# A Mamba and mixture-of-experts block on one core: who makes the products with C, and when ScalarE empties the banks of the last batch

## What is computed

```python
def _mamba_dir(xz, conv_w, conv_b, xproj_w, dtproj_w, dt_bias, A_log, Dp):
    ...
    dA = jnp.exp(jnp.einsum('bdl,dn->bdln', delta, A))
    dBx = jnp.einsum('bdl,bnl,bdl->bdln', delta, Bm, u)
    h = _ssm_scan(dA, dBx)
    y = jnp.einsum('bdln,bnl->bdl', h, Cm)
    y = y + Dp[None, :, None] * u
    return y * jax.nn.silu(z)
...
xz = jnp.einsum('ed,bld->bel', in_proj_w, hidden_states)
out_f = _mamba_dir(xz, ...)
out_b = _mamba_dir(xz[:, :, ::-1], ...)[:, :, ::-1]
attn = jnp.einsum('bdl,od->blo', out_f + out_b, out_proj_w)
...
w = jax.nn.softmax(topv, axis=-1)               # 4 of 16 experts for a token
hidden = jax.nn.gelu(jnp.einsum('bld,efd->blef', x, w1) + b1, approximate=False)
exp_out = jnp.einsum('blef,edf->bled', hidden, w2) + b2
fused = jnp.sum(w[..., None] * jnp.take_along_axis(exp_out, topi[..., None], axis=2), axis=2)
```

## Time and profile before

| | |
|---|---|
| median of 3 runs | 1203.09 us (1200.37 to 1204.73) |
| the profiled execution's own time | 1202.14 us |
| its span in the profile | 1200.2 us |
| mean granted TensorE clock | 0.925 |
| busy, share of the span | DVE 90%, PE 79%, ACT 76%, POOL 73% |
| DMA | 222.64 MB, 185 GB/s |

### The profile page before, as it was taken

The page is one execution under the profiler, slowest core; times in us unless marked ns, Lnnn a source line. Parts: engine busy times, 40 slices in busy tenths (PEclk is TensorE's granted clock), DMA queues, the critical chain, the costliest instruction groups (busy, mean ns, idle before and its releaser), DMA issues. The chain is left out here.

```text
span 1200.2 us, 21505 instructions
## 1 busy us (share of the span) xinstructions
PE 948.7 (79%) x5691; PEld 752.3 (63%) x5764; DVE 1083.1 (90%) x1402; ACT 910.8 (76%) x1647; POOL 874.9 (73%) x530
## 2 busy tenths in 40 slices
PE   5267788854789888988898888889888888897872
PEld 5133243323678767877777677777777767776762
DVE  7886788849999999999999989999999999698952
ACT  2037887777799987989898888889898987878720
POOL 1077868773579878987897788789878878785562
PEclk9987877776899999999999999999999998899985
DMA  9924445568556866776676668667766766554455
GB/s 314 325 82 156 176 154 218 186 250 294 178 168 170 228 184 168 199 198 178 162 218 185 190 151 228 166 170 201 203 171 165 230 177 170 141 146 144 118 108 152
DMA packets 151298, 222.64 MB, mean 185 GB/s; under 512 B 36028, under 2 KB 97756, under 8 KB 146276
## 3 DMA queue, kind: packets, MB, share of 16 engines
q1 hardware_dynamic: 124036, 202.16, 52.6%
q0 software_dynamic: 27136, 19.02, 11.1%
HBM read 159.74 MB, written 65.52 MB: 188 GB/s over the span
## 5 line engine op out<-in xcount | busy, mean ns | idle before, releaser
L748 POOL TENSOR_TENSOR arena<-arena 128x1024 f32<-128x1024 f32 x227 | 494.2, 2332 | 147.3 <-DVE arena L1390 131.7
L1390 DVE TENSOR_TENSOR_SCAN arena<-arena,ps 128x512 f32<-128x512 f32 x512 | 601.0, 1205 | 0.1
L934 ACT ACTIVATE arena<-delta,a_neg 128x511 f32<-128x511 f32 x512 | 338.2, 723 | 4.2 <-issue 2.2
L733 POOL DMA_INDIRECT acc_d<-yrows,tags x160 | 255.2, 1595 | 54.3 <-issue 36.1
L1083 PE MATMUL ps<-ident,arena 128*128 128x128 f32 x2048 | 275.8, 279 | 7.0 <-POOL arena L748 4.7
L1378 DVE TENSOR_TENSOR ps<-du,ps 128x512 f32<-128x512 f32 x384 | 253.8, 676 | 10.1 <-issue 5.8
L1083 PEld LDWEIGHTS ps<-ident,arena 128*128 128x128 f32 x2048 | 238.1, 144 | 17.6 <-POOL arena L748 4.7
L1112 PE MATMUL ps<-w,arena 128*128 128x128 f32 x1248 | 177.6, 286 | 10.5 <-DVE arena L1390 5.4
L715 POOL DMA_INDIRECT slots_d<-arena,pos x128 | 154.2, 1205 | 42.1 <-issue 40.6
L1104 PE MATMUL ps<-rowsT,w 128*128 128x256 f32 x640 | 159.1, 393 | 8.9 <-ACT arena L885 7.1
L1112 PEld LDWEIGHTS ps<-w,arena 128*128 128x128 f32 x1248 | 155.2, 194 | 15.1 <-ACT yrows L880 5.3
(11 more groups left out here) (141 smaller groups left out, 944.5 us busy)
## 6 DMA issues: line engine op xcount, KB each, us to landing
arena<-c_d SPq DMA_DIRECT2D x128, 512.0 KB
w<-w_dram SPq DMA_DIRECT2D x80, 258.0 KB
w<-w_dram SPq DMA_DIRECT2D x80, 256.0 KB
rows<-slots_d SPq DMA_DIRECT2D x80, 130.0 KB
slots_d<-delta SPq DMA_DIRECT2D x5, 2015.0 KB, 20.2
delta_d<-arena SPq DMA_DIRECT2D x8, 1024.0 KB
du_d<-delta SPq DMA_DIRECT2D x8, 1024.0 KB
delta<-delta_d SPq DMA_DIRECT2D x8, 1024.0 KB, 7.3
```

The source lines that it names most:

```text
L733: pool.indirect_dma_start(acc_d, bass.IndirectOffsetOnAxis(ap=tags[:, j, a, 0:1].bitcast(I32), axis=0), yrows[:, j % W_RING, a, :], None, ...
L748: nc.gpsimd.tensor_tensor(state[:, q % H_RING], state[:, q % H_RING], c_rows[:, r % C_RING], ALU.mult).then_inc(s["prod_done"], 1)
L934: nc.scalar.activation(decay[:, q % DA_RING, j, lo:lo + L - 1], delta[:, par, dh, lo:lo + L - 1], ACT.Exp, scale=a_neg[:, dh, 2 * g + j:2 ...
L1390: nc.vector.tensor_tensor_scan(state[:, q % H_RING, j, way], decay[:, q % DA_RING, j, way], b_ps[:, ROW[q, j], j, way], 0.0, ALU.mult, ALU ...
```

## The change

Three tables change, and one call is added.

- `VECTOR`: in a middle batch VectorE makes the product of pair 16 only, where it made those of pairs 8, 16 and 24.
- `LAST_VECTOR`: in the last batch VectorE makes the products of pairs 22 to 31, where it made those of 13, 16, 18, 20, 22, 24, 26 and 28. So that pair 31 can be among them, a call behind the loop over the pairs is added.
- `LAST_STEP`: in the last batch ScalarE empties the banks of TensorE's step p in step p+2, p+3 or p+4, where it was p+4 throughout (steps 12, 13, 24 and 25 are emptied within the GELU bursts, as before).

All other pairs' products are GpSimd's. The number of products, emptyings and sends stays what it was.

```diff
--- before.py
+++ after.py
@@ -58,8 +58,8 @@
 
 
 FIRST_VECTOR = (1, 4, 7)
-VECTOR = (8, 16, 24)
-LAST_VECTOR = (13, 16, 18, 20, 22, 24, 26, 28)
+VECTOR = (16,)
+LAST_VECTOR = tuple(range(22, 32))
 
 
 def vector_pairs(b):
@@ -158,7 +158,9 @@
 LAST_LAG = 4
 LAST_GELU = [16, 28]
 LAST_BURSTS = [[12, 13], [24, 25]]
-LAST_EMPTY = [[p for p in range(2, PAIRS) if p + LAST_LAG == q and p not in LAST_BURSTS[0] + LAST_BURSTS[1]]
+LAST_STEP = [p + (LAST_LAG - 2 if p < 6 or 15 < p < 19 else LAST_LAG - 1 if p < 9 or 13 < p < 22 or p == 26 else
+                  LAST_LAG - 2 if p > 26 else LAST_LAG) for p in range(PAIRS)]
+LAST_EMPTY = [[p for p in range(2, PAIRS) if LAST_STEP[p] == q and p not in LAST_BURSTS[0] + LAST_BURSTS[1]]
               for q in range(PAIRS + LAST_LAG)]
 
 
@@ -1419,6 +1421,8 @@
                     product(q + 2)
                     scan(q + 3, 0)
                     scan(q + 3, 1)
+                if isinstance(b, int) and b == BATCH - 1:
+                    product(PAIRS - 1)
 
             batch(0, 0, 0)
             batch(1, 1, 0)
```

## The result

The changed kernel takes 1166.84 us in the median of four runs (1161.03 to 1173.30); the kernel before took 1203.91 us beside it (1200.37 to 1205.13). The ratio is 0.972, with a 95% interval of 0.968 to 0.976: faster by 37 us. The forecast was 1164 us. The profiled execution of the changed kernel is the slowest of the four (1173.3 us, span 1170.8), so the two profiles differ by less than the medians: 1200.2 - 1170.8 = 29.4 us.

A forecast was written before the change was run, and what follows sets the result against it. VectorE was taken to bound the middle batches, chained scatters the end. 22.3 + 7.2 + 4.1 + 2.5 + 2.8 = 38.9 us off 1202.1 gives 1163.2, as median 1164; 8-in-10 range 1157 to 1181.

The forecast's parts named there:

- Removed products, 22.3 us: Six middle batches: VectorE loses the products of pairs 8 and 24, 1.14 + 2.58 us a batch, 22.3 us saved.
- The kept product, +7.2 us: Middle batches: pair 16's product on VectorE falls from 2.66 to 1.22 us in five batches, 7.2 us saved.
- VectorE comes first by 0.7 us, and the 1.44 us are not paid: Middle batches: VectorE starts pair 16's product at 6.2 us, before GpSimd is free for pair 15 at 6.9.
- an unfavourable phase: Last batch: a 4.33 us product showed that unfavourable phases could make the middle batches' kept product longer.
- Rival (a): Middle batches: the kept product goes on meeting GpSimd, 31.7 us gained in all, 1171 us; chance 0.28.
- TensorE and GpSimd follow at no cost: Middle batches: GpSimd's 98 us of work fits under VectorE's 103.6, TensorE's margin barely holds; the move costs nothing.
- Start of the last batch, 4.1 us: Before the last batch's gatings: earlier emptying gives 3.2 us, a kept clock up to 1.7 more; 4.1 taken.
- Middle of the last batch, 2.5 us: Last batch after the gatings: only TensorE's own gain counts, bounds 2.1 and 3.9 us, 2.5 taken.
- TensorE's wait under 3: Middle of the last batch: TensorE's wait of 4.69 us would fall to under 3 in the new profile.
- End of the last batch, 2.8 us: Last batch's sends: first 4.0 us later, third at 1127.7 instead of 1130.47, 2.8 us gained; bounds -1 and 6.
- every pair of sends 8 us apart: End of the last batch: each send waits for the one before to land, 8 us apart before and after.

The follow-up runs named there:

- the two halves' runs: mid_only and last_only, each one half of the change on the kernel before: 1183.63 us and 1187.40 us.
- again: The changed kernel run once more, unaltered: 1168.26 us, ratio 0.972 to the kernel before.
- kept_none: The changed kernel without any VectorE product in the middle batches, GpSimd makes all 32: 1148.40 us, ratio 0.953 to the kernel before.
- last_only: The changed kernel with the old VECTOR list (8, 16, 24), so only the last batch is changed: 1187.40 us, ratio 0.986 to the kernel before.
- mid_only: The kernel before with VECTOR = (16,), so only the middle batches are changed: 1183.63 us, ratio 0.983 to the kernel before.
- lv_only: The kernel before with only the new list of last-batch VectorE products (pairs 22 to 31): 1202.79 us, ratio 0.998 to the kernel before.
- ls_only: The kernel before with only the new LAST_STEP table (earlier evictions in the last batch): 1198.12 us, ratio 0.990 to the kernel before.
- kept_19: The changed kernel with the middle batches' remaining VectorE product moved from pair 16 to pair 19: 1157.35 us, ratio 0.965 to the kernel before.
- kept_8: The changed kernel with the middle batches' remaining VectorE product moved from pair 16 to pair 8: 1157.37 us, ratio 0.963 to the kernel before.
- no_reload: The changed kernel without SyncE's reload of the scans' sums beside the last sends: 1173.99 us, ratio 0.975 to the kernel before.

## Why the prediction was right, and where it was not

The direction, the bound (VectorE in the middle batches, the chain of sends at the end) and the total were right: 37 us measured, 38.9 forecast. Most of the terms were not.

**Removed products, 22.3 us: right.** Twelve products fewer; the two halves' runs and the group agree once the kept product is set apart.

**The kept product, +7.2 us: wrong, and this is the step that failed** ("VectorE comes first by 0.7 us, and the 1.44 us are not paid"). The arithmetic ahead of it came out in the fifth middle batch: VectorE issues the product 6.1 us behind the scans of pair 14 (854.86 to 861.00; forecast 6.2), GpSimd is free for pair 15 at 861.9, 7.0 behind (forecast 6.9). VectorE came first by 0.9 us there and by 0.7 at 645.99 (3.85 us long); in the other four batches it came 0.1 to 0.4 us after GpSimd had become free (2.67 to 2.97 us long), and in `again` it came first in all six, by 0.1 to 1.0. So the margin of 0.7 us was too thin to forecast the order by. Above all, coming first is not enough: the product behind GpSimd's scatter went ahead, and VectorE waited for the rest of the scatter and for all of it. The row that shows this, 4.33 us at 1086.10, was in the trace of before, and the prediction took it for an unfavourable phase. In place of a gain of 7.2 us the runs show a loss of 3.4 (19.4 instead of 16.0 us for six) to 6.0 (22.0). Rival (a), which had the product unchanged at 2.66, was nearer for this term and still too kind. The Trainium skill (SBUF — State Buffer, Who interferes with whom) says that two such instructions exclude each other for a whole instruction and that issue order decides. The exclusion agrees with every row here (1.1 us of VectorE's own work behind the end of GpSimd's product: 864.97 after 863.88); the order of issue that the rows list does not decide in the case at 861.00.

**TensorE and GpSimd follow at no cost: right.** Outside the loop's edge VectorE waits 1.1 us in six middle batches, and `kept_none` moves six more products to GpSimd without a wait of VectorE.

**Start of the last batch, 4.1 us (bounds 3.2 and 4.9): under-sized**, 6.6 in the profile. `last_only` has the same 2.5 us of idle time before the gatings, `mid_only` still 7.7, so it comes from the last batch's part of the change; of its two halves `lv_only`, which leaves the evictions as before, still has 8.3, and `ls_only` 5.0 in its one profile. TensorE's wait fell from 4.93 to 1.41 us, 3.5 (forecast 3.2). Most of the rest is the clock. TensorE's windows of the changed kernel there show the high level throughout, where before it was granted 0.50 for 3.4 us:

```profile
1022.00:1025.00 3.00, 1.59 (x15) 1.58 (x15) 3.00 (x5) 3.00 (x9) 3.00 (x2) 1.00 0.98 226
1025.00:1028.00 3.00, 3.00 (x26) 2.63 (x24) 0.62 (x2) 1.52 (x4) 2.86 (x2) 1.00 0.45 132
```

From the transpose to the second gating it takes 4.7 us instead of 7.0 (1023.42 to 1028.09, before 1042.69 to 1049.72), 2.4 us less. I had taken half of 1.7 us for the clock into the sum, and the 1.7 was itself too small. The last 0.7 us of the 6.6 I haven't traced.

**Middle of the last batch, 2.5 us (bounds 2.1 and 3.9): the clock decides.** The first profile gives 0.9, `again` 3.2 (second gating to the scans of pair 16, 51.8 us before, 50.9 and 48.6). Both have TensorE idle for 2.67 or 2.68 and then 0.68 us; in the first its clock then falls, in the second not. The same two gaps stand in four more profiles: the clock falls in `kept_19` and stays in `kept_8`, `kept_none` and `last_only`. The windows, first the changed kernel, then `again`:

```profile
1068.00:1072.00 4.00, 2.59 (x16) 2.33 (x16) 3.14 (x4) 3.26 (x7) 3.77 (x3) 0.79 0.49 150
1072.00:1076.00 4.00, 3.66 (x16) 3.51 (x17) 0.00 (x0) 0.66 (x2) 1.22 (x1) 0.50 0.59 185
```

```profile
1064.00:1068.00 4.00, 3.00 (x25) 2.84 (x26) 2.38 (x3) 3.17 (x7) 4.00 (x3) 1.00 0.41 140
1068.00:1072.00 4.00, 4.00 (x31) 3.71 (x29) 2.98 (x4) 2.09 (x5) 0.74 (x1) 1.00 0.56 188
```

VectorE's wait after it is 4.92 us in the one and 2.65 in the other. The 3.2 us of `again` lie within the forecast's bounds, the 0.9 of the first profile below them; the announced sign "TensorE's wait under 3" came true in both.

**End of the last batch, 2.8 us: under-sized**, 6.8 in the profile and 6.1 in `again`. The first send was later and the third earlier, as forecast. Too small was what follows: I had every pair of sends 8 us apart before and after. That figure came from three rows, and the trace of before goes on with 7.0 and 6.0 (GpSimd):

```profile
1154.39 1.57 POOL L733 DMA_INDIRECT acc_d<-yrows,tags  x1 [1.54 <-DMA acc_d<-yrows,tags]
1161.42 1.57 POOL L733 DMA_INDIRECT acc_d<-yrows,tags  x1 [1.56 <-DMA acc_d<-yrows,tags]
1167.45 1.58 POOL L733 DMA_INDIRECT acc_d<-yrows,tags  x1 [0.55 <-issue]
```

In the changed kernel sends four to seven go 2.4 to 2.6 us behind the end of the issue before, some 6.1 us apart, with C rows and weights still read between them. What the slow rows of before have and these have not is a weight load that SyncE issues during the second scatter of the send (1133.66 and 1140.49; the next sends go 4.21 and 4.25 us behind that scatter's end). That this is the cause was not tried by a run. `no_reload` shows that the one gap of 9 us is a read. From the third send to the tenth it is 45.5 us (before 49.0), and the third comes 14.8 behind the first (forecast 16). The VectorE products beside the sends cost little: a scatter that is issued while one of them works takes up to 1.05 us longer (2.60 instead of 1.55 in `again`), once or twice in a run, and a scatter that runs already when the product is issued takes no longer (1.55 at 1130.84, with the product at 1131.68).

**The sum.** 38.9 - 10.6 (kept product) + 2.5 (start) - 1.6 (middle) + 4.0 (end) - 3.6 (edge, and 1.1 of small waits in the middle batches) gives 29.6, the first profile's 29.4. Of that, 2.9 us of the edge and 2.3 of the clock in the middle are chance. The rest of the way to the 37 us between the medians isn't traced to one place; the stretch before the first gating, which the change doesn't touch, ended between 386.0 and 395.1 us in the profiles of these kernels (in that of `ls_only` at 406.1), so the times of single executions spread by as much. That 1164 was so near is luck: the middle batches were forecast some 10 us too good and the last batch 5 to 8 too poor.

## What to carry to other kernels

A product that one engine keeps is worth moving to where the other engine's queue is empty: the same instruction cost 1.2 us at pair 19, 1.2 to 2.3 at pair 8 and 2.7 to 4.1 at pair 16, and giving all to the slower engine (94% busy, still ahead of need) was best, 18 us below the change. Look for such contention in the mean length of an instruction's group, since no wait is booked for it.

When a margin of under 1 us decides a term, weigh the rival's value into the sum, and test the parts apart: a total that fits can hide errors of 5 to 10 us in each direction. A spacing read off three rows of a chain holds only for those three; read the chain to its end. And a row that doesn't fit the rule in use, as the 4.33 us, is worth following on the other engine before the forecast.

## What the runs showed of the hardware

- A GpSimd product that is ready behind a scatter goes ahead of a VectorE product issued up to 1.2 us before the scatter ends (4.33 us at 1086.10 of the kernel before, 3.97 at 861.00 of the changed one, instead of 1.22). Without a product ready behind it, a scatter does not hold VectorE up (1.22 at 852.23 of `kept_19`, 1.21 at 1131.68 of the changed kernel). Why the queued product wins wasn't tried by itself; the lengths of GpSimd's instructions in the trace are rough.
- The other way round, a scatter issued while a VectorE product works is lengthened by about what is left of the product (0.3 us at 853.02 of `kept_19`, where 0.43 were left, 1.05 at 1103.09 of `again`, where 1.17 were left). A scatter that began before the product keeps its 1.55 to 1.58 us.
- Three GpSimd products of 128x1024 in a row take 6.48 to 6.64 us, of which 0.57 lie under the scatter before: 2.0 each, at any load seen here, up to 94% of its time.
- TensorE's granted clock fell to the 1.2 GHz level after 2.67 us idle and a further 0.68 in two profiles (the changed kernel and `kept_19`), and stayed at 2.4 GHz after the same gaps in four (`again`, `kept_8`, `kept_none`, `last_only`). A forecast that hangs on this can only give both values, here 2.3 us apart.
- At the end of the last batch, where a send waits for nothing but the landing of the one before, it goes 2.4 to 2.8 us behind the end of that one's second scatter (from the fourth send on, in the changed kernel, `again` and `no_reload`), and 5.4 and 5.75 us behind it with the read of 1.75 MB beside it (`again` and the changed kernel); without that read (`no_reload`) no wait is over 2.8.
